# Two-layer GNN kernel: 73 tiles instead of 74 in the edge-tile loop, accumulators turned by one place

## The reference

```python
feat = concatenate([n_f[edge_src], n_f[edge_dst]], axis=1)
e_ho = relu(feat[E_HH + E_OO:] @ W_ho + b_ho)          # 7424 of the 8192 edges
logit = (e_f @ W_a + b_a)[:, 0]
alpha = softmax of logit over the edges of each target
z_f = segment_sum(alpha[:, None] * n_f[edge_src], edge_dst)
new = relu(concatenate([n_f, z_f], axis=1) @ (W_hn or W_on) + b)
```

## Time and profile before

| | us |
|---|---|
| median of three runs | 372.44 |
| the profiled execution's own time | 373.84 |
| its span (first to last instruction) | 371.7 |
| TensorE busy (matmul) | 327.9 |
| VectorE busy | 293.2 |
| ScalarE busy | 195.8 |
| POOL busy | 134.6 |

### The profile page before, as it was taken

How to read it: one execution, slowest core, us unless ns; L and a number is a source line. 1 busy time by engine, 2 the same in 40 slices (tenths; PEclk the granted TensorE clock), 3 DMA queues, 4 the chain that set the end, 5 groups by cost and what they waited for, 6 DMA issues and landing times.

```text
span 371.7 us, 4709 instructions
## 1 busy us (share of the span) xinstructions
PE 327.9 (88%) x1440; PEld 252.5 (68%) x1440; DVE 293.2 (79%) x411; ACT 195.8 (53%) x300; POOL 134.6 (36%) x203
## 2 busy tenths in 40 slices
PE   2999999999999997999999999872989998699580
PEld 1778877676646885888888888741777875588230
DVE  0799999949699786999999999797765667746535
ACT  3755495211044336977877775525156577343145
POOL 4300070281005400699898777472004331050000
PEclk9999999999999998999999999988699999699786
DMA  7998699799989990001101100142443996000002
GB/s 230 408 407 316 220 321 316 252 289 258 363 291 335 383 402 4 0 2 71 45 0 48 69 2 2 56 131 94 167 174 145 328 327 218 0 2 0 1 0 113
DMA packets 17640, 63.11 MB, mean 170 GB/s; under 512 B 2235, under 2 KB 2237, under 8 KB 17361
## 3 DMA queue, kind: packets, MB, share of 16 engines
q1 hardware_dynamic: 13520, 50.07, 36.9%
q0 software_dynamic: 2096, 8.74, 8.0%
q10 hardware_dynamic: 2000, 4.00, 3.0%
HBM read 59.64 MB, written 3.16 MB: 169 GB/s over the span
## 4 chain that ended last, share of the span: by engine, by line
PE 69%; DVE 21%; ACT 4%; issue 2%; DMA 2%; POOL 1%; SPq 0%; DVEq 0%; ACTq 0%
PE ps L1288 21%; PE ps L1135 10%; PE ps L1179 7%; PE ps L1384 7%; PE ps L1322 5%; DVE W_lo L707 4%; PE ps L1330 4%; PE ps L1295 3%; PE ps L1154 3%; PE ps L1354 3%; DMA x_nat<-in_x_dram 2%; PE ps L1410 2%; ACT W_hi L445 1%; DVE tile_val L728 1%; PE ps L1211 1%
## 5 line engine op out<-in xcount | busy, mean ns | idle before, releaser
L445 ACT CAST W_hi<-W_raw 128x1024 fp32r<-128x1024 f32 x72 | 73.2, 1046 | 63.1 <-DMA W_raw<-in_L_gnn_W_ho_dram 24.6
L943 DVE SCALAR_TENSOR_TENSOR ps<-ps,wa_bc 128x1024 f32<-128x1024 f32 x74 | 87.6, 1257 | 2.9 <-PE ps L1288 2.7
L707 DVE TENSOR_TENSOR W_lo<-W_raw,W_hi 128x1024 fp32r<-128x1024 f32 x58 | 70.7, 1243 | 21.2 <-ACT W_hi L445 18.2
L1288 PE MATMUL ps<-A_tab,oh 128*128 x148 | 53.7, 444 | 2.2 <-ACT oh L554 2.2
L372 POOL TENSOR_TENSOR W_lo<-W_raw,W_hi 128x1024 fp32r<-128x1024 f32 x14 | 35.4, 2538 | 48.3 <-ACT W_hi L445 48.3
L398 POOL TENSOR_SCALAR sc_r<-irow,keys 128x64 f32<-128x64 f32 x74 | 35.1, 474 | 39.9 <-PE ps L1295 39.8
L1288 PE MATMUL ps<-B_tab,oh 128*128 x148 | 47.0, 399 | 0.0
L1135 PE MATMUL ps<-W_hi,xT_hi 128*128 128x512 f32 x112 | 46.4, 414 | 0.6 <-DVE W_lo L707 0.6
L1135 PE MATMUL ps<-W_lo,xT_hi 128*128 128x512 f32 x112 | 44.2, 395 | 0.0
L560 ACT ACTIVATE sc_l<-sc_l,keys 128x64 f32<-128x64 f32 x74 | 24.5, 341 | 20.9 <-DVE ps L943 14.5
L1135 PE MATMUL ps<-W_hi,xT_lo 128*128 128x512 f32 x112 | 35.0, 394 | 0.0
(11 more groups left out here) (242 smaller groups left out, 548.1 us busy)
## 6 DMA issues: line engine op xcount, KB each, us to landing
W_raw<-in_L_gnn_W_oo_dram SPq DMA_DIRECT2D x8, 1024.0 KB, 9.8
W_raw<-in_L_gnn_W_ho_dram SPq DMA_DIRECT2D x8, 1024.0 KB, 5.2
W_raw<-in_L_gnn_W_hh_dram SPq DMA_DIRECT2D x8, 1024.0 KB, 8.6
W_raw<-in_L_gnn_W_hn_dram SPq DMA_DIRECT2D x8, 1024.0 KB, 5.0
W_raw<-in_L_gnn_W_on_dram SPq DMA_DIRECT2D x8, 1024.0 KB, 5.0
W_raw<-in_L_gnn_W_dram SPq DMA_DIRECT2D x4, 1024.0 KB, 4.9
key_rows<-key_rows_scratch POOLq DMA_DIRECT2D x1, 2304.0 KB, 14.3
table_scratch<-tabs ACTq DMA_DIRECT2D x2, 1024.0 KB, 6.6
```

Source lines behind the costliest of these rows:

```text
L445: sa.copy(W_hi[:, ring(n), :], W_raw[:, n // 2 % NS, n % 2, :]).then_inc(hi_made, 1)
L707: v.tensor_tensor(W_lo[:, ring(n), :], W_raw[:, n // 2 % NS, n % 2, :], W_hi[:, ring(n), :].bitcast(F32), ALU.subtract).then_inc(lo_made, 1)
L943: v.scalar_tensor_tensor(acc, acc, 0.0, wa_bc[:], ALU.max, ALU.mult, accum_out=keys[:, t, 2:3]).then_inc(reduced, 1)
L1288: ins = mm(acc[:, n * 512:(n + 1) * 512], oh[:, t // 2 % 2, k, t % 2 * P:(t % 2 + 1) * P], tab[:].rearrange("p q d -> p (q d)")[:, n * 512 ...
```

## The change

The number of tiles and the size of the arrays are now two names: `NL` = 73 is how many tiles every loop runs over, and `NT` = 74 stays the size of the arrays and the number of tiles for which one-hot matrices are made. All four engines run over `NL` tiles, and every wait for the end of the loop asks for `NL`. Tile t uses accumulator 1 + (t + 2) % 3 where it used 1 + t % 3. Before, the last tiles 71, 72, 73 had accumulators 3, 1, 2; now the last tiles 70, 71, 72 have accumulators 1, 2, 3. The wait ahead of chunks 48 and 49 is rewritten to match: it asked for 73 reductions (tile 72) and now asks for 71 (tile 70).

```diff
-NT = -(-(JH + NC - 1) // 2) * 2
+NL = JH + NC - 1
+NT = -(-NL // 2) * 2
...
-            for t in range(NT):
+            for t in range(NL):
                 ends(t)
...
-            pool.wait_ge(gathered, NT)
+            pool.wait_ge(gathered, NL)
...
-            for t in range(NT - 4, NT):
+            for t in range(NT - 4, NL):
                 scale_ends(t)
-            act.wait_ge(gathered, NT)
+            act.wait_ge(gathered, NL)
...
-            act.wait_ge(scattered, 1 + JO + NT)
+            act.wait_ge(scattered, 1 + JO + NL)
...
             def reduce_tile(t):
-                acc = ps[:, (1 + t % NG) * D:(2 + t % NG) * D]
+                acc = ps[:, (1 + (t + 2) % NG) * D:(2 + (t + 2) % NG) * D]
...
-            for t in range(NT):
+            for t in range(NL):
                 reduce_tile(t)
-            dve.wait_ge(scattered, 1 + JO + NT)
+            dve.wait_ge(scattered, 1 + JO + NL)
...
-                acc = ps[:, (1 + t % NG) * D:(2 + t % NG) * D]
+                acc = ps[:, (1 + (t + 2) % NG) * D:(2 + (t + 2) % NG) * D]
...
-            for t in range(NT):
+            for t in range(NL):
                 of_source, of_target, column, _ = load(t)
...
-                        pe.wait_ge(reduced, NT)
+                        pe.wait_ge(reduced, NL)
...
             pe.wait_ge(both_made, 4)
-            pe.wait_ge(reduced, NT - (NT - 1) % NG)
+            pe.wait_ge(reduced, NL - (NL + 1) % NG)
             update(END["hoB"], END["hoB"] + 2)
-            for t in range(NT - LAG, NT):
+            for t in range(NL - LAG, NL):
                 scatter(t, load(t + LAG)[2])
```

## The result

| | before | after |
|---|---|---|
| median (lowest to highest), nine runs each, us | 372.28 (370.12 to 374.27) | 370.35 (369.17 to 371.47) |
| ratio after / before, 95% interval | | 0.9943 [0.9915, 0.9972] |
| the profiled execution's own time / span | 373.84 / 371.7 | 369.17 / 367.2 |
| VectorE busy, TensorE busy | 293.2, 327.9 | 292.1, 322.2 |

Between the medians the kernel is 1.93 us faster, 0.52%; between the means of the nine runs (372.28 and 370.16 us), from which the ratio comes, it is 0.57%. 1.75 us were forecast. The two profiled executions differ by much more, 4.5 us of span: the one of before lies near the top of its range, the one of after at the bottom. Most of what follows is how to take the 1.75 us out of those 4.5.

The account below looks back on a forecast made before the run. VectorE was taken to bound the loop at 1.185 us a tile. The sum 1.18 (tile) + 0.93 (wait) - 0.04 (scaling) - 0.32 (bias DMAs) = 1.75 us gave 370.7 us from 372.44, range 368.5 to 372.8.

Parts of the forecast that it names:

- One tile, 1.18 us: In the tile loop, leaving out tile 73 starts VectorE's last reduction 1.18 us earlier.
- The wait, 0.93 us: Ahead of chunk 48, the wait asks for tile 70's reduction, already past: its first weights gain another 0.93 us.
- Scaling just in time, 0.04: The last scatter needs tile 72's scaled one-hot matrix, ready just in time: 0 to 0.1 us charged, 0.04 taken.
- Bias DMAs uncovered, 0.32: ScalarE's two bias DMAs ahead of the counts' copy now end after the scatters, taking back 0.32 us.
- POOL passes the gain on: After the counts' copy, the start of POOL's four subtractions sets the mean logits' end, 1.75 us earlier.
- Turned accumulators and the rest, 0: Other accumulators at the loop's start and for chunks 50 and 51, and everything behind the softmax: zero gain or loss.
- The idle time before the transposes keeps its length: TensorE's idle 6.51 us before the softmax's transposes was to stay as long, said against a slower clock in z.
- One of the prediction's own signs of being wrong: The time from the transposes (L1344) to the span's end, 112.5 us, changing by more than 1 us.
- only the tile: At the loop's end, the wait's 0.93 us come back at the last scatter or in register loads: 371.3 us, chance 0.17.
- The ports one place earlier: VectorE gets the shared ports ahead of a POOL subtraction, at L878 or L970: 2.2 us less, 368.5 us, chance 0.15.
- The clock low through the second half of z: From 261 to 275 us, z's second half at 1.2 GHz takes 2.90 us more: 373.6 us, chance 0.08.

Follow-up runs that it names:

- the second pair: Second traces of the kernel before and the changed kernel, both unchanged, one run each: 373.29 us before and 369.39 us after.
- the first experiment: 73 tiles with accumulators not turned, against the kernel before: 373.06 us, ratio 1.0032 [1.0008, 1.0057].

## Why the prediction was right

- *One tile, 1.18 us:* right, reductions at 1.182 us. It stood in the sum, and as a rival, as if it paid by itself. It does not: unturned, 73 tiles gain nothing.
- *The wait, 0.93 us:* chunk 48's weights went from 0.19 behind the last reduction's start to 0.79 ahead of it, 0.98 us.
- *Scaling just in time, 0.04:* 0.14 us (eight weight loads in 1.23 in place of 1.09). The step was right: the scaling ended at 232.38 + 0.35 = 232.73, and the last pair's first weights came 0.12 us behind it, at 232.85, where even spacing would have had them at 232.70. The size lay above the 0 to 0.1 us that were charged.
- *Bias DMAs uncovered, 0.32:* 0.28, shown by moving them.
- *POOL passes the gain on:* right. L879 to L881 took 2.48, 2.47, 2.77 us; the last ended at 246.53, 0.54 us behind POOL's fourth subtraction (235.96 + 10.03 = 245.99), as before (249.28 against 248.73), and the experiments moved both. The rule of the Trainium skill (SBUF — State Buffer, section SBUF: two separate sides), that VectorE and GpSimd lock their shared ports for a whole instruction, agrees: the same three instructions took 0.69, 0.43 and 0.75 us with POOL still.
- *Turned accumulators and the rest, 0:* right as far as the traces can tell; the loop's start stays open, as said above.
- *The idle time before the transposes keeps its length:* it did not, it went from 6.51 to 7.87 us. The first half of z was not slower for it (5.65 us against 6.62).

The sum is 1.18 + 0.98 - 0.14 - 0.28 = 1.74 us against 1.75. The terms are off by 0.05, 0.10 and 0.04 us, and that these cancel to 0.01 is luck. The measured 1.93 has an interval of 1.0 to 3.2 us, so the traces and not the medians bear out the terms. One of the prediction's own signs of being wrong came up: the time between the transposes and the span's end was to change by no more than 1 us, and it went from 112.46 to 110.71, 1.75 us less. The sign was set too tight, for the kernel before alone differs by 1.27 us there between its two traces (112.46 and 111.19); in the second pair the change is 0.40 us. So it does not speak against the terms, but neither do the traces rule out a small share of the change behind the transposes.

Of the rivals, *only the tile* fell: at the last scatter 0.14 of the 0.98 us came back and no more, and in the first experiment the tile alone gave nothing. *The ports one place earlier* did not happen: L879 was ready at 238.74, 0.4 us behind the start of POOL's second subtraction (238.30); about 0.3 had been worked out. *The clock low through the second half of z* did not happen either; that half took 3.72 us in each trace.

## What to carry to other kernels

Where a loop ends in a wait on a chosen buffer, count which iteration the wait asks for: an iteration less can leave it asking for the very same event and pay nothing, and turning the buffers makes it pay. Here one tile less alone was 0.3% slower, and with the turning 0.6% faster. Measure a small gain in two traces from the nearest event that both share, here the last reduction, and not from the span. When an engine's work is moved earlier, look at what stands in the queues ahead of its consumers, here two DMA issues of 1.1 us.

## What was not expected of the hardware

Idle time of TensorE can cost twice: behind 2.12 us of it ahead of chunk 48 the clock was 0.63 and 0.52 in the next stretches and four scatters took 0.95 us more, while behind 0.89 us before it stayed at 1.00. And the earlier transposes of one version were partly given back by a first half of z at 5.26 us, where a version with TensorE busy up to them had 3.72. Not every gap does this: in the kernel after TensorE was busy for 1.20, 1.20 and 0.50 us of the three stretches of 2 us from 238 to 244, and the clock stayed at 1.00 until 252.

Not every VectorE instruction waits for POOL: the reciprocal of the same size (L878, at 235.36) took 3.35 us beside POOL's first subtraction, and 3.35 us with POOL still.
